# A last slot of three blocks, its key rows stored in two parts, and a last pair in two pieces, in a two-layer graph kernel

## The reference

```python
x = _layernorm(x + L0(x, edge_index, edge_attr_16, ...))   # attention: softmax over the edges of a node, 4 heads
x = _layernorm(x + L1(x, edge_attr_128, edge_index, edge_weight1, Wq, Wk, Wv))

# L0: alpha = leaky_relu(a_src.x_i + a_dst.x_j + a_edge.ef); e = exp(alpha - max over the node's edges)
#     out = segment_sum(x_j * e / sum(e)); out = elu(layernorm(out + bias + x))
# L1: alpha = sum(q[dst] * w * k[src]) / 4 * cutoff; out = segment_sum(alpha * v[src])
```

## Time and the profile before

| | us |
|---|---|
| median of 3 runs | 4164.89 (4162.8 to 4166.21) |
| the profiled execution, its time | 4166.46 |
| the profiled execution, its span | 4164.8 |
| granted TensorE clock over the span | 0.592 |

### The profile page before, as it was taken

How to read it: one execution, slowest core, us unless ns; L and a number is a source line. 1 busy time by engine, 2 the same in 40 slices (tenths; PEclk the granted TensorE clock), 3 DMA queues, 4 the chain that set the end, 5 groups by cost and what they waited for, 6 DMA issues and landing times.

```text
span 4164.8 us, 43395 instructions
## 1 busy us (share of the span) xinstructions
PE 1931.6 (46%) x10576; PEld 1624.9 (39%) x10576; DVE 2554.3 (61%) x4276; ACT 256.5 (6%) x646; POOL 3064.1 (74%) x3247
## 2 busy tenths in 40 slices
PE   4644445545444555544524444444444444444444
PEld 2433234333232333333424444444444444444444
DVE  3555555655555566555656666666666666676666
ACT  1101101100111110001100000000000000000000
POOL 7777777777777777777357777777777777777775
PEclk6666666776666676766755555555555555555555
DMA  8444445444444544444256666666666666666664
GB/s 207 132 135 118 120 125 140 128 140 125 121 119 121 139 131 137 125 127 119 77 193 222 211 222 216 215 223 213 223 212 212 223 215 222 214 219 219 210 222 134
DMA packets 357908, 711.10 MB, mean 171 GB/s; under 512 B 126483, under 2 KB 214548, under 8 KB 344676
## 3 DMA queue, kind: packets, MB, share of 16 engines
q0 software_dynamic: 129504, 324.46, 28.4%
q1 hardware_dynamic: 181880, 354.74, 25.5%
q10 hardware_dynamic: 46476, 31.39, 2.4%
HBM read 682.18 MB, written 28.15 MB: 171 GB/s over the span
## 4 chain that ended last, share of the span: by engine, by line
POOL 40%; issue 19%; DVE 14%; DVEq 13%; PE 9%; DMA 4%; ACT 1%; POOLq 0%; SPq 0%; ACTq 0%
POOL ring L1323 27%; POOL ring L576 13%; DVEq L913 5%; DVE work L916 5%; PE psum L1352 4%; DMA ring<-kv_table,den_cols 2%; PE psum L698 2%; DVE ring L1516 1%; DVEq L1503 1%; DVEq L1498 1%; DVEq L1507 1%; DVEq L73 1%; DMA dst_pair<-dst_row_dram 1%; DVE work L1013 1%; DVE work L1016 0%
## 5 line engine op out<-in xcount | busy, mean ns | idle before, releaser
L576 POOL DMA_INDIRECT ring<-x_table,idx x1584 | 1499.5, 947 | 483.0 <-issue 459.9
L1323 POOL DMA_INDIRECT ring<-kv_table,den_cols x1516 | 1433.3, 945 | 461.8 <-issue 452.0
L1352 PE MATMUL psum<-work,ring 128*128 128x42 f32 x3232 | 712.4, 420 | 425.1 <-DVE ring L1516 425.1
L1352 PEld LDWEIGHTS psum<-work,ring 128*128 128x128 f32 x3232 | 697.0, 332 | 454.0 <-DVE ring L1516 454.0
L1494 DVE TENSOR_TENSOR psum<-psum,ring 128x2048 f32<-128x2048 f32 x101 | 232.3, 2300 | 584.5 <-DMA ring<-kv_table,den_cols 550.9
L698 PE MATMUL psum<-work 128*42 128x132 f32 x3232 | 491.1, 316 | 189.5 <-DVE work L1016 189.5
L1345 PE MATMUL psum<-ring,work 126*128 126x128 bf16 x1616 | 190.7, 312 | 702.3 <-DVE ring L1500 678.3
L698 PEld LDWEIGHTS psum<-work 128*42 128x42 f32 x3232 | 412.9, 137 | 246.4 <-DVE work L1016 220.4
L1345 PEld LDWEIGHTS psum<-ring,work 126*128 126x128 bf16 x1616 | 164.1, 146 | 718.1 <-DVE ring L1500 693.4
L916 DVE TENSOR_TENSOR work<-dst_pair,psum 126x1024 bf16<-126x1024 int32 x204 | 249.2, 1221 | 74.9 <-issue 43.0
L1016 DVE TENSOR_TENSOR work<-ring,psum 128x1056 f32 (+1 forms) x202 | 251.3, 1244 | 0.0
(11 more groups left out here) (202 smaller groups left out, 2076.7 us busy)
## 6 DMA issues: line engine op xcount, KB each, us to landing
dst_pair<-dst_row_dram SPq DMA_DIRECT2D x204, 512.0 KB
dst_pair<-dst_row_dram SPq DMA_DIRECT2D x101, 1024.0 KB
ring<-ea_dram SPq DMA_DIRECT2D x101, 1024.0 KB, 5.5
ring<-x_table,idx POOLq DMA_INDIRECT x1584
ring<-kv_table,den_cols POOLq DMA_INDIRECT x1516, 2.8
ea_pair<-ea_turned_dram SPq DMA_DIRECT2D x102, 128.0 KB
kv_table<-work ACTq DMA_DIRECT2D x17, 512.0 KB, 3.1
q_table<-work ACTq DMA_DIRECT2D x17, 384.0 KB, 3.9
```

Of the source, the lines that this page charges most:

```text
L576: pool.indirect_dma_start(x_rows[:, h * CHUNK_TILES + t, :], None, k["x_table"], bass.IndirectOffsetOnAxis(idx[h][:, t:t + 1], 0))\
L1323: pool.indirect_dma_start(kv[p % BUFS][:, t, :], None, k["kv_table"], bass.IndirectOffsetOnAxis(index[:, tile:tile + 1], 0))\
L1352: last = pe.matmul(sum_ps[u], message[e][:, u * GROUP + t, :], onehot[e][:, u * GROUP + t, :], start=t == 0, stop=t == GROUP - 1)
```

## The change

Slots of the last chunk are of three blocks (384 nodes) instead of four, in both layers. The count of passes takes this in: the last chunk's span gets its own count, and the larger one is used. In the last slot of layer 0 the keys and values are made before the queries and stored in two parts, 256 rows and 128 rows. POOL, before it starts layer 1, waits for both. The last pair of layer 1 is taken in two pieces, 8 tiles and 4 tiles, each with its own semaphore for its gathers; PE sums the first piece while DVE works on the second. The roots of layer 1's last slot are made by POOL instead of by three Newton steps on DVE. In the last `maxima` PE runs six products of zeros while it waits for the exponentials, and five after it.

```diff
+FIN_LAST = 3
+LAST_MUL, LAST_SHIFT = 43, 14
...
-def rows_start(eng, reg, fin_row, slot, pass_no):
+def rows_start(eng, reg, fin_row, slot, pass_no, nb):
...
-    eng.reg_add(reg, reg, pass_no * FIN_NODES)
-    eng.reg_alu(reg, reg, NODE_ROWS - FIN_NODES, op=ALU.min)
+    eng.reg_add(reg, reg, pass_no * (nb * P))
+    eng.reg_alu(reg, reg, NODE_ROWS - nb * P, op=ALU.min)
...
         dve.tensor_reduce(out=fin_passes, in_=fin_span, axis=AX.X, op=ALU.max)
+        dve.tensor_scalar(last_passes, fin_span[:, CHUNKS - 1:CHUNKS], FIN_LAST * P - 1, None, ALU.add)
         dve.drain()
         dve.tensor_scalar(fin_passes, fin_passes, FIN_NODES - 1, None, ALU.add)
+        dve.tensor_scalar(last_passes, last_passes, LAST_MUL, None, ALU.mult)
         dve.drain()
         dve.tensor_scalar(fin_passes, fin_passes, 9, None, ALU.arith_shift_right)
+        dve.tensor_scalar(last_passes, last_passes, LAST_SHIFT, None, ALU.arith_shift_right)
+        dve.drain()
+        dve.tensor_tensor(out=fin_passes, in0=fin_passes, in1=last_passes, op=ALU.max)
         dve.drain()
         dve.tensor_tensor(out=passes_sb, in0=passes_sb, in1=fin_passes, op=ALU.max).then_inc(prologue_over, 1)
...
+        def busy(n):
+            for _ in range(n):
+                pe.matmul(k["bank"][7][0:ROWS, :], zeros[:, 0:ROWS], zeros, start=True, stop=True)
...
+            if keep_busy:
+                busy(6)
             pe.wait_ge(exp_done, s + 1)
...
+            if keep_busy:
+                busy(5)
...
-        finish()
+        finish(True)
...
+            if last_slot:
+                for half, half_out in enumerate((kv_out, kv_last_out)):
+                    copy_key_values(v, half, nb)
+                    act.drain()
+                    n = min(2, nb - 2 * half)
+                    act.dma_start(k["kv_table"][bass.DynSlice(start + half * 2 * P, n * P), :]
+                                  .rearrange("(b p) f -> p b f", p=P),
+                                  kv_rows[:, half * FIN_NODES:half * FIN_NODES + n * 2 * FEAT].rearrange("p (b f) -> p b f", b=n))\
+                       .then_inc(half_out, 16)
+                copy_query(v, nb)
...
+            with pool.Fori(0, passes) as again:
+                wait_here(pool, var_made, pool.snap(last_visit) + 1, pool_gate)
+                root = rstd[:, 0:FIN_LAST]
+                pool.tensor_tensor(out=root, in0=root, in1=k["half_neg"][:, 0:FIN_LAST], op=ALU.pow).then_inc(pool_root_made, 1)
+                pool.reg_add(last_visit, last_visit, 1)
...
+        def last_pair(e, buf, group, uses, turn, r, sums_of):
+            for u in range(2):
+                n = LAST_TILES_OF[u]
...
+                dve.wait_ge(last_kv_in[u], 16 * n * (r + 1))
...
+                if u == 0:
+                    dve.wait_ge(summed, turn)
+                    add(sum_ps[0], sums_of[0])
+                    dve.drain()
+                    add(sum_ps[1], sums_of[1]).then_inc(added, 1)
```

More of the change, by code:

```diff
@@ L721, in turn_slot, with key_values @@
             wait_here(pe, x1T_copied, v + 1, pe_gate)
-        def key_values(half):
-            for u in range(2):
+        def key_values(half, nb):
+            for u in range(min(2, nb - 2 * half)):
                 b = 2 * half + u
@@ L734, in query, with finish @@
             last.then_inc(q_made, 1)
-        def finish():
+        def finish(last_slot=False):
             with pe.Fori(0, passes) as r:
                 v = pe.snap(fin_visit)
-                turn_slot(v)
-                query()
+                nb = FIN_LAST if last_slot else FIN
+                turn_slot(v, nb)
+                if not last_slot:
+                    query(nb)
                 for half in range(2):
-                    key_values(half)
+                    key_values(half, nb)
+                if last_slot:
+                    query(nb)
                 pe.reg_add(fin_visit, fin_visit, 1)
@@ L772, in on_tensor @@
             finish()
-        maxima(CHUNKS - 1)
+        maxima(CHUNKS - 1, True)
         with pe.Fori(0, passes) as r:
@@ L842, in finish_slot @@
             act.wait_ge(x1_turned, v + 1)
-            act.activation(x1T, y_ps, ACT.Copy).then_inc(x1T_copied, 1)
-            act.wait_ge(q_made, v + 1)
-            act.activation(q_rows[:, :, 0, :], blocks(q_ps), ACT.Copy).then_inc(q_part_copied, 1)
-            for half in range(2):
-                act.wait_ge(kv_made, 2 * v + half + 1)
-                act.activation(kv_rows[:, half * FIN_NODES:(half + 1) * FIN_NODES], kv_ps[half], ACT.Copy)
-            act.drain()
-            act.dma_start(rows_of(k["kv_table"]), kv_rows.rearrange("p (b f) -> p b f", b=FIN)).then_inc(kv_out, 16)
+            act.activation(x1T[:, 0:nodes], y_ps[:, 0:nodes], ACT.Copy).then_inc(x1T_copied, 1)
@@ new lines, in finish_slot @@
+            if last_slot:
+                for half, half_out in enumerate((kv_out, kv_last_out)):
[7 more added lines that the diff above has]
+                copy_query(v, nb)
+            else:
+                copy_query(v, nb)
+                for half in range(2):
+                    copy_key_values(v, half, nb)
+                act.drain()
+                act.dma_start(rows_of(k["kv_table"]), kv_rows.rearrange("p (b f) -> p b f", b=FIN)).then_inc(kv_out, 16)
@@ L1259, in layer1 @@
     root_made = S("root1_made")
+    var_made = S("var1_made")
+    pool_root_made = S("pool_root1_made")
     rows_made = S("rows1_made")
@@ L1354, in sums, with last_sums, finish @@
             last.then_inc(summed, 1)
-        def finish():
+        def last_sums(n, e, r):
+            wait_here(pe, rows_made, pe.snap(fin_visit) + 1, pe_gate)
+            pe.wait_ge(last_made, r + 1)
+            for u in range(2):
+                if u:
+                    pe.wait_ge(msg_made, n + MSG_CREDIT + 1)
+                to = last_sum_ps if u == 0 else sum_ps[1]
+                for t in range(LAST_TILES_OF[u]):
+                    last = pe.matmul(to, message[e][:, u * GROUP + t, :], onehot[e][:, u * GROUP + t, :],
+                                     start=t == 0, stop=t == LAST_TILES_OF[u] - 1)
+                last.then_inc(last_summed if u == 0 else summed, 1)
+        def finish(nb=FIN):
             with pe.Fori(0, passes) as r:
@@ L1364, in finish, with chunk @@
                 pe.reg_add(fin_visit, fin_visit, 1)
-        def chunk(pairs, slot_due, last_chunk=False):
+        def chunk(pairs, slot_due, last_chunk=False, r=None):
             n = pe.snap(done)
@@ L1373, in chunk @@
                     finish()
-                sums(n + i, i % 2)
+                if last_chunk and i + 1 == pairs:
+                    last_sums(n + i, i % 2, r)
+                else:
+                    sums(n + i, i % 2)
             pe.reg_add(done, done, pairs)
@@ L1413, in finish @@
                 act.drain()
-                act.dma_start(rows_of(k["out"]), blocks(o)).then_inc(written, 16)
+                act.dma_start(rows_of(k["out"]), blocks(o, nb)).then_inc(written, 16)
                 act.reg_add(fin_visit, fin_visit, 1)
```

215 lines of the change are left out of this document (138 added, 77 removed).

## The result

The changed kernel takes 7520.68 us (median of 4 runs, 7515.78 to 7526.87), the kernel before it 4164.27 beside it (4 runs, 4162.8 to 4166.21): 1.8054 times, 95% interval 1.8033 to 1.8076. The forecast was 7520.

A forecast was written before the change was run, and what follows sets the result against it. POOL was taken to be bound by its own gather instructions. With two passes, 4164.8 + 37 + 1193 + 46 + 19 + 28 + 2015 + 19 - 0.5 = 7521, forecast 7520 us, range 7380 to 7670 (0.81).

The forecast's parts named there:

- (a): Ahead of the first chunk, layer 0: scores of 12 more groups, bound by transfers and not hidden, +37 us.
- (b): 16 chunks of layer 0: second messages and second slot visit on DVE, 193.8 us a chunk, +1193 us.
- (c): Last chunk and slot of layer 0: second messages and visit, 61.8 us, less the edits' gains, +46 us.
- (d): Layer 1, first pass: second visit at each of 16 slots stalls POOL, 1.2 us taken each, +19 us.
- (e): Layer 1, turn between passes: POOL starts over 28 us after its last gather, +28 us.
- (f): Layer 1, second pass: 2014.8 + 19 us, and its end with edits and second visit, -0.5 us.
- The count: Passes worked out on chip: last span 443 nodes against 384 rows gives two; one pass had chance 0.05.
- the room of 17.7 a chunk: Layer 0: DVE's wait for POOL per chunk, too small to hide the addition of 92 us; hiding had chance 0.02.
- The dearer rival: Layer 0 messages: PE's clock at its lower level through both runs, 544 us more, 8060; over 7670 chance 0.06.
- the cheaper one: Layer 0 messages near DVE's busy time, 16 x 14 us less, 7300; under 7380 with two passes chance 0.06.
- a step that failed: Layer 1, first pass: DVE, busy some 13 of 20 us a pair, makes up its delay of 11 in two pairs.
- The 1.4 for a raised clock: Last chunk of layer 0: products of zeros raise PE's clock before the first group of sums, saving 1.4 us once.

The follow-up runs named there:

- one-pass kernel: Changed kernel with the last span counted to 6250 nodes, so one pass, and zeros stored in the last 128 key rows; ratios 0.9954, 0.9966, 0.9969 to the kernel before.

## Why the prediction was right

The terms, each against the changed kernel's trace, in us:

| | predicted | measured | from |
|---|---|---|---|
| (a) scores ahead of chunk 0 | +37 | +36.7 | 168.9 less 132.2 |
| (b) 16 chunks | +1193 | +1208.5 | 3116.2 less 1907.7 |
| (c) last chunk and slot | +46 | +47.9 | 3285.1 to 3410.6, less 77.6 |
| (d) layer 1, first pass | +19 | +3.9 | 3410.6 to 5429.3, less 2014.8 |
| (e) the turn | +28 | +33.7 | 5429.3 to 5463.0 |
| (f) second pass and end | +2033.5 | +2025.6 | 5463.0 to 7521.1, less 32.5 |
| sum | +3356.5 | +3356.3 | |

**The count** was read rightly: 443 nodes against 384, one shift, two passes. One number in one `memset` takes the loss away, and one in the kernel before brings it in. Both are shown, by ratios to the kernel before beside them, and the counts of 408 and 3032 show it in the changed kernel's own trace.

**Layer 0 is not hidden** (b): the room of 17.7 a chunk could not take 92 more. The chunk came out 1.0 longer than the forecast 193.8. The messages were the largest unknown. Their two runs in windows, as the earlier trace rows:

```profile
3107.20:3161.00 53.80, 38.95 (x264) 29.74 (x264) 39.78 (x73) 3.28 (x12) 40.62 (x44) 0.93 0.62 178
3161.95:3215.90 53.95, 41.75 (x264) 31.76 (x264) 39.82 (x72) 3.28 (x12) 13.46 (x15) 0.87 0.44 136
```

The clock was 0.93 and 0.87 where it was 0.81 before, PE was busy 39 and 42 where it was 44, and each run took the same 54. Between 0.81 and 0.93 PE's clock does not set their time. The dearer rival's condition, the lower level through both runs, did not arise, so its price stays untested; the cheaper one, messages near DVE's busy time, did not come either.

**Layer 1** (d) was over-sized. A doubled visit in the first pass, from ACT's first norms to the gather that waits for the sums:

```profile
3572.52 1.50 ACT L1483 ACTIVATE ring<-psum,ring 128x128 f32<-128x128 f32 x4 [13.10 <-DVE ring L1594]
...
3575.70 0.40 ACTq L1475 DMA_DIRECT2D ring<-x_table  x1
3576.44 0.63 ACT L1478 ACTIVATE ring<-sumT 128x512 f32 x1 [2.42 <-issue]
...
3578.09 6.89 PE L1410 MATMUL psum<-work,ring 128*128 128x42 f32 x32
...
3585.82 0.94 POOL L1375 DMA_INDIRECT ring<-kv_table,den_cols  x1 [0.44 <-issue]
```

The mechanism is the predicted one, but the load follows 3.2 behind the norms (3.6 forecast) and the sums end 9.3 behind the load (9.5), 0.6 less in all. The gather stood idle for 0.44 instead of 0.30, a stall of 0.14 where 0.8 was worked out and 1.2 taken. The first pass grew by 3.9, 0.24 a slot, and the second by 7.8; both are inside the bounds of 0 and 6 a slot. Together that is 26 us less than the sum had, and 15.5 more in (b), 5.7 in (e), 3.5 in the end and 1.9 in (c) cancel it. The exact hit is luck; the terms by themselves were off by up to 16 us, 0.2% of the time.

**The turn** (e) hides a step that failed, though it is written under (d): "DVE, busy some 13 of 20 us with a pair, makes up its own delay of 11 in two pairs". Behind a doubled visit DVE needs 16 us a pair (L1614 at 5402.46 and 5418.47, no wait for its rows noted at either), as it waits in each for the sums of the pair before. So it gains 4 of POOL's 20 a pair, and the last chunk has five pairs in all. When the last gather ends, the pair before the last one should be in its sums for 2.2 us; here they start 3.3 after it (5432.64), 5.5 late. DVE has the roots 21.8 after the last gather against 28.2 before, 6.4 less and not 11. The second visit took 9.2 from root to root where 10.9 was forecast. And POOL's first gather follows its second root by 2.95 us for which the profile shows no wait (2.7 from DVE's taking up the root); this piece of the turn stood in no term. So 4.6 more, 1.7 less and 2.7 more make 33.7 out of 28. The end of the second pass is longer for like reasons, 35.5 where 32 was forecast: the roots at 19.9 and not 17, the second visit 9.3, and 6.3 behind it where the kernel before has 4.3.

**The edits' own gain** (c): predicted were 9.4 in the visit that POOL waits for, measured are 35.7 - 27.8 = 7.9 in the changed kernel and 8.8 in the one-pass kernel; the 0.9 between them is PE's 9 products at the start of the visit, at 0.50 in the changed kernel. The sum came out near, but its terms did not. The prediction let the visit end with the landing of the last store, took the 8.5 us from its issue to the gather for that landing, and took 3 off for a smaller store. In fact the landing left the chain altogether, and DVE's work on the queries took its place, as shown above. So the small store gives nothing, the three blocks give 4.6 to 5.9 and not 3.6, and the order gives 2.9 to 4.2 where 2.8 was forecast, mostly because the landing no longer counts. The 1.4 for a raised clock did not come.

On the clock the Trainium skill, TensorE: Matmul & The Clock Gate, in its part on the clock gate, holds that sustained matmul activity releases it. The windows above agree for the sums: 3.4 us of fp32 products in one piece are followed by 0.96. The eleven bf16 products ran in two stretches of 2.75 and 2.32 us, with smaller products and breaks between and behind them, and no rise followed, whether they read 1 row or 126. Whether this speaks against the section can't be told from it, as no run made the products one piece.

## What to carry to other kernels

When a buffer or a slot is made smaller, look first for the arithmetic that counts how often it must be visited, and put the real numbers of the inputs through it: here 443 against 384 doubled every loop for a block's worth of savings. Where such a count is shared by the whole kernel, one tight place sets it for all; the last span was counted to the padded end of the table, and counting to the 6250 real nodes keeps the one pass and the gain. So does leaving the slot at four blocks, within the spread of these runs. A count of instructions in the profile tells such a thing sooner than any time. And when a store's landing is the last wait of a stretch, look for the wait behind it before making the store smaller: here two semaphores were waited for one after the other, and the second took over.

## What was not expected of the hardware

The same kernel took 4164 where the changed kernel was measured, and 5070, 5058 and 4996 beside the three sets of experiments. The record names chip 6 for the first two sets and chip 7 for the third, and no chip for the 4164; whether the chip itself makes the difference was not separated from anything else. POOL's gathers are as fast there (945 to 949 ns). What comes late is the release of those that wait for PE's sums while gathers run. Over all pairs, DVE's adds of such sums waited 842.6 us (90 times) in the kernel with its last pair whole, and 7.7 us (twice) in the kernel before at 4164. From the former, two sets of the same 32 products and DVE's add behind each; POOL's last gather started at 4999.96:

```profile
4989.27 7.05 PE L1415 MATMUL psum<-work,ring 128*128 128x42 f32 x32 [4.22 <-issue]
5004.10 0.20 DVE L1539 TENSOR_TENSOR sumT<-sumT,psum 128x42 f32 x1 [10.48 <-remote]
...
5013.13 7.05 PE L1415 MATMUL psum<-work,ring 128*128 128x42 f32 x32 [4.09 <-DVE ring L1638]
5020.32 0.20 DVE L1539 TENSOR_TENSOR sumT<-sumT,psum 128x42 f32 x1 [5.04 <-PE psum L1415]
```

It is 14.8 us from the first product to the add with gathers under way up to 5000.9, and 7.2 without gathers. In the changed kernel, measured where the kernel before takes 4164, the gather that waits for such sums starts 7.1 after the first product, with gathers under way:

```profile
3524.88 7.06 PE L1410 MATMUL psum<-work,ring 128*128 128x42 f32 x32 [4.21 <-DVE ring L1636]
3531.99 0.95 POOL L1375 DMA_INDIRECT ring<-kv_table,den_cols  x1 [0.30 <-PE psum L1410]
```

With two passes in layer 0 it is worse. POOL gathers a chunk there without a break, as its paced waits count events that now come twice, and in the kernel with layer 1 once two of ACT's copies of the sums came one 33 us after its first product (3143.05) and the next 67 us after that, 4 us after the end of the chunk's last gather (start 3238.07):

```profile
3176.08 0.27 ACT L837 ACTIVATE work<-psum 42x132 f32<-42x132 f32 x1 [35.79 <-remote]
3243.28 0.27 ACT L837 ACTIVATE work<-psum 42x132 f32<-42x132 f32 x1 [66.92 <-remote]
```

That makes a chunk of two passes 288 us there ((4862.2 - 255.5) / 16) instead of 194.8. The one-pass kernel there takes 143.6 a chunk instead of 119.2, and 16 times the difference, 2309, is most of the 2394. Why PE's results come late in the one place and not in the other stays open; the rows show only that they are late while gathers run, and on time when they stop. The forecast of 7520 holds for the first place alone; by the two kernels with one layer twice, the change would be slower in the other too, at an estimated 10016 us.
